# Macaron block on one core: the low parts of k and q ahead of the routing pieces, and ScalarE normalising the rows at the head of a batch's fifth step

## The reference

```python
def _layernorm(x, axis=-1, eps=1e-05):
    m = jnp.mean(x, axis=axis, keepdims=True)
    v = jnp.var(x, axis=axis, keepdims=True)
    return (x - m) / jnp.sqrt(v + eps)
...
# attention: 16 heads of 64; x is (8, 512, 128)
scores = jnp.einsum('bach,baCh->bacC', k, q)
masked = jnp.where(causal, scores, jnp.float32(-MASK_VAL))
attn = jax.nn.softmax(masked / np.float32(np.sqrt(D_HEAD)), axis=-1)
z = jnp.einsum('bacC,baCh->bach', attn, v)
out = jnp.einsum('aeh,bach->bce', W_O, z)
...
x = x + 0.5 * _L0_ffn_ref(_layernorm(x, axis=-1), ...)
x = x + _L0_attn_ref(_layernorm(x, axis=-1), ...)
x = x + 0.5 * _L0_ffn_ref(_layernorm(x, axis=-1), ...)
```

## Time and profile before

| | |
|---|---|
| Median of three runs | 929.5 us (927.78 to 931.06) |
| The profiled execution's own time | 929.25 us |
| Its span in the profile | 927.2 us |
| Busy share of the span | PE 96%, PEld 83%, DVE 84%, ACT 76%, POOL 30% |
| TensorE's granted clock | 0.995 of full speed on average |

### The profile page before, as it was taken

The page is one execution under the profiler, slowest core; times in us unless marked ns, Lnnn a source line. Parts: engine busy times, 40 slices in busy tenths (PEclk is TensorE's granted clock), DMA queues, the critical chain, the costliest instruction groups (busy, mean ns, idle before and its releaser), DMA issues.

```text
span 927.2 us, 25462 instructions
## 1 busy us (share of the span) xinstructions
PE 887.6 (96%) x7882; PEld 771.4 (83%) x7882; DVE 777.9 (84%) x3083; ACT 705.5 (76%) x2040; POOL 281.4 (30%) x328
## 2 busy tenths in 40 slices
PE   7999999979999999999999999999999998999995
PEld 6889999867887887887887887787788787999995
DVE  7878888779799889799889889979988986786666
ACT  3787667578887878787878787878887786887881
POOL 5777203142121021322222322310200202667552
PEclk9999999999999999999999999999999999999998
DMA  9677556155666575556456556554545454557758
GB/s 250 218 223 248 181 161 194 59 158 132 171 162 170 148 187 153 174 149 170 151 164 143 173 143 173 145 173 133 173 127 167 139 174 152 169 159 211 222 155 237
DMA packets 141300, 157.43 MB, mean 170 GB/s; under 512 B 35328, under 2 KB 108832, under 8 KB 141168
## 3 DMA queue, kind: packets, MB, share of 16 engines
q1 hardware_dynamic: 128256, 135.53, 50.1%
q0 software_dynamic: 8352, 18.17, 8.1%
q10 hardware_dynamic: 4560, 2.12, 0.8%
HBM read 97.53 MB, written 58.23 MB: 168 GB/s over the span
## 4 chain that ended last, share of the span: by engine, by line
PE 67%; DVE 15%; issue 6%; DMA 5%; POOL 3%; ACT 2%; SPq 2%; DVEq 0%; POOLq 0%; ACTq 0%
PE psum L2497 12%; PE psum L2382 8%; PE psum L2552 8%; PE psum L2538 7%; PE psum L2333 6%; PE psum L2335 5%; PE psum L2334 5%; PE psum L2561 5%; PE psum L2568 5%; DVE arena L1955 3%; POOL x_slots L852 2%; DVE arena L1970 2%; PE psum L2221 2%; PE psum L2355 1%; PE psum L2345 1%
## 5 line engine op out<-in xcount | busy, mean ns | idle before, releaser
L1125 ACT ACTIVATE arena<-arena,neg_max 128x512 f32<-128x512 f32 (+3 forms) x512 | 281.7, 554 | 108.2 <-DVE neg_max L1955 108.2
L1955 DVE CUSTOM_DVE_ANT_0 arena<-psum,causal 128x512 f32<-128x512 f32 (+3 forms) x512 | 217.1, 480 | 41.0 <-PE psum L2497 39.8
L1069 ACT ACTIVATE arena<-psum,b_t 128x256 f32<-128x256 f32 (+1 forms) x336 | 121.0, 443 | 38.8 <-PE psum L2335 29.2
L871 POOL DMA_INDIRECT arena<-y_tiles,y_at x64 | 61.7, 964 | 270.9 <-PE psum L2497 189.0
L2382 PE MATMUL psum<-w_sb,arena 128*128 x1136 | 140.8, 275 | 0.1
L2382 PEld LDWEIGHTS psum<-w_sb,arena 128*128 128x128 f32 x1136 | 134.2, 192 | 0.3 <-issue 0.3
L852 POOL DMA_INDIRECT x_slots<-xr,slot x64 | 62.1, 971 | 234.7 <-PE psum L2497 188.6
L2538 PEld LDWEIGHTS psum<-ident,arena 128*128 128x128 f32 x776 | 86.9, 141 | 17.8 <-ACT arena L1125 6.6
L2538 PE MATMUL psum<-ident,arena 128*128 128x128 f32 x776 | 95.9, 273 | 4.5 <-DVE arena L1985 4.1
L1135 ACT ACTIVATE arena<-psum 128x512 f32<-128x512 f32 x192 | 99.2, 587 | 0.6 <-PE psum L2538 0.6
L1125 ACT ACTIVATION_READ_ACCUMULATOR arena<-arena,neg_max 128x1 f32 x512 | 97.8, 191 | 0.0
(11 more groups left out here) (363 smaller groups left out, 2024.5 us busy)
## 6 DMA issues: line engine op xcount, KB each, us to landing
turned_dram<-arena SPq DMA_DIRECT2D x252, 128.0 KB
y_all<-turned_dram SPq DMA_DIRECT2D x63, 512.0 KB, 4.1
arena<-inv_dram SPq DMA_DIRECT2D x128, 128.0 KB, 3.9
w_raw<-in_L_ffn_W_dram SPq DMA_DIRECT2D x60, 256.0 KB
xg<-x_slots SPq DMA_DIRECT2D x43, 144.0 KB
arena<-in_L_ffn_W_dram SPq DMA_DIRECT2D x24, 256.0 KB
arena<-y_rows SPq DMA_DIRECT2D x16, 256.0 KB, 4.9
y_tiles<-y_all SPq DMA_DIRECT2D x27, 128.0 KB, 1.9
```

The source lines that it names most:

```text
L1069: ins = act.activation(h_t[side(f, n)][:, k, 0:rows], H_BANKS[side(f, n)][k // 2][:, k % 2 * rows:(k % 2 + 1) * rows], ACT.Relu, bias=b1_t ...
L1125: ins = act.activation(prob_tile(i, h, t), prob_tile(i, h, t), ACT.Exp, scale=-1.0, bias=neg_max[i % 2][:, h, t:t + 1], accum_out=row_sum[ ...
L1955: ins = dve.tensor_tensor_reduce(out=prob_tile(i, h, t), in0=score_tile(t, h), in1=causal[:, SEQ - (t + 1) * P:SEQ], scale=-1.0, scalar=-2 ...
```

## The change

The splits of the next step's k and q move ahead of the first four pieces of a step (in the step before the last, ahead of all that are finished there). `norms(b)` no longer normalises: it waits until ScalarE has read the values of the batch before, computes `moments` as before, and one product, `shift` = -mean x rstd. Step 3 finishes what is left. ScalarE normalises with activations of the kind Identity (scale `rstd`, bias `shift`), one for each tile of 128 rows, four tiles for `xa` and four for `xr1`, at the head of step 4, ahead of that step's exponentials.

```diff
-        TURN_STEP, PUT_STEP, JOIN_STEP = 4, 4, 5
+        TURN_STEP, PUT_STEP, JOIN_STEP, NORM_STEP = 4, 4, 5, 4
...
+            def normalise_rows(b, dst, col, ready):
+                for n in range(QT):
+                    ins = act.activation(dst[:, n, 0:D], xs[:, b * QT + n, :], ACT.Identity, bias=shift[:, col + n:col + n + 1],
+                                         scale=rstd[:, col + n:col + n + 1])
+                ins.then_inc(ready, 1)
+
+            def normalise_for(b):
+                act.wait_ge(norm_ready, U1 + b + 1)
+                if b + 1 < BATCH:
+                    normalise_rows(b + 1, xa[(b + 1) % 2], 0, xa_ready)
+                if b > 0:
+                    if b - 1 >= 2:
+                        act.wait_ge(x_put[b - 3], SCATTERED)
+                    normalise_rows(b - 1, xr1[(b - 1) % 2], QT, xr_ready)
...
+                    if s == NORM_STEP:
+                        normalise_for(b)
                     exps(i, 3)
...
                 if b > 0:
                     yield from measure(batch_of(b - 1), QT)
-                yield from moments(slice(0 if b + 1 < BATCH else QT, 2 * QT if b > 0 else QT))
-                if b + 1 < BATCH:
-                    yield from normalise(batch_of(b + 1), xa[(b + 1) % 2], 0, xa_ready)
                 if b > 0:
-                    yield from second_rows(b - 1, QT)
+                    dve.wait_ge(xa_ready, b + 1)
+                if b > 1:
+                    dve.wait_ge(xr_ready, BATCH + b - 1)
+                tiles = slice(0 if b + 1 < BATCH else QT, 2 * QT if b > 0 else QT)
+                yield from moments(tiles)
+                dve.scalar_tensor_tensor(out=shift[:, tiles], in0=mean[:, tiles], scalar=-1.0, in1=rstd[:, tiles],
+                                         op0=ALU.mult, op1=ALU.mult).then_inc(norm_ready, 1)
+                yield
...
                         turn_long(i)
+                    if i + 1 < STEPS:
+                        split_k(i + 1)
+                        split_q(i + 1)
                     if i == STEPS - 2:
                         finish(work)
                     go_on(work, 4)
-                    if i + 1 < STEPS:
-                        split_k(i + 1)
-                        split_q(i + 1)
...
                     go_on(work, 5)
+                    if s == NORM_STEP - 1:
+                        finish(work)
```

## The result

The changed kernel takes 939.62 us (median of four runs, 938.2 to 941.96), against 930.28 us of the kernel before (927.78 to 931.37): the ratio is 1.0107, 95% interval 1.0076 to 1.0137. It is 9.3 us slower. The profiled execution took 939.29 us beside a span of 937.6 us, that is 10.0 us over the profiled execution of before, where 7.8 us were forecast. The two spans differ by 10.4 us.

A forecast was written before the change was run, and what follows sets the result against it. Steps were taken as TensorE's own 8.88 us plus delays paced by a chain through three engines. 5 x 1.31 + 1.17 + 0.6 = 8.3 us, less 0.5, gave 7.8 over 929.25: 937.0 us, range 933 to 940.5.

The forecast's parts named there:

- What bounds the kernel: Step heads: 0.36 us is the ordinary cost of turning to the next step; only time beyond TensorE's 8.88 us is winnable.
- the 18.7 us: TensorE's weight loads, listed as waiting for q_lo in 35 places; rival (a) took these waits as real, faster, chance 0.08.
- ScalarE's block: Head of step 4, batches 1 to 6: eight activations overfill 1.66 us idle; 1.31 us a batch, 1.17 in batch 1.
- the two delays: Step 5's later scores (0.84 us) and later low part of activations (1.31 us); rival (c) had them add, 943 us, chance 0.06.
- VectorE's relief: VectorE loses 56 normalisations, 15.5 us in all; at most some 1.1 us in step 4, which the block holds longer anyway.
- The splits: VectorE's two subtractions ahead of up to four pieces: counted at nothing, at most 1.4 us gained, with a loss near the end.
- The 0.23 us of step 2: Batch 3: the part of TensorE's 0.60 us wait for q_lo that earlier splits free, but that isn't kept.
- so these come when they did: Steps 3 and 4: VectorE has no idle time before their maxima, so their starts, and step 4, stay unchanged.
- The step before the last: The rest of the routing falls behind the splits, delaying count_bf, last scores and last maxima; 0.6 us loss, between 0 and 1.2.
- Batches 0 and 7: Their four activations take 1.54 us and fit in idle time; both together counted at nothing, bounds -1.0 and +0.5.
- What would show it: Signs expected in the changed profile, among them step 4 0.8 us longer, step 5 0.5, and q_lo's sum down over 10 us.
- slower tiles: Upper bound of the range: ScalarE's block tiles taking 0.03 us more for each of 8 x 6, 1.4 us.

The follow-up runs named there:

- split_only: The kernel before with only the splits moved ahead of the four pieces, VectorE still normalising; 995.13 us, ratio 1.0036 to the kernel before.
- norm_only: The changed kernel with the splits put back behind the pieces, ScalarE still normalising; 998.94 us against 991.84 of the kernel before, ratio 1.0069.
- half: The changed kernel, but ScalarE normalises only the four tiles of xa and VectorE those of xr1; 992.38 us, ratio 1.0006 to the kernel before.
- two_steps: The changed kernel with ScalarE's tiles divided, xa heading step 4 and xr1 step 5 (batch 7: step 4); 991.74 us, ratio 0.9989 to the kernel before.
- twelve: The changed kernel with four more, unused activations at the head of step 4 in batches 1 to 6; 1007.68 us, ratio 1.0224 to the kernel before.
- spread: two_steps with the splits back behind the pieces and pieces redistributed over steps in batches 1 to 6; 976.69 us against 984.89 of the kernel before, 0.9915.
- after_again: The changed kernel, unchanged, profiled again on another chip; 995.13 us against 984.89 of the kernel before, ratio 1.0096.
- before_again: The kernel before, unchanged, profiled again as the control on the other chip; 986.36 us in one run.

## Why the prediction was right

**What bounds the kernel.** Right. The 0.36 us at the heads was the price of the turn; only the label went from q_lo to "issue". split_only shows that none of the 18.7 us could be had. The prediction says that nearly all of the 35 gaps are of that length: 25 are within 0.01 us of it. Of the other ten two are long, 2.7 and 2.0 us in steps 1 and 2 of batch 0, and the change left these as they were.

**ScalarE's block.** Right in mechanism and size. 0.385 us a tile and 3.08 us for eight, against 0.386 and 3.09; step 4's exponentials 4.07 us behind the head against 2.77, 1.30 us later (forecast 1.31). norm_only shows it by itself, 1.29 us a batch against 1.31, and half, two_steps and twelve bracket it: four tiles cost nothing, eight 1.3 us, twelve 1.53 us more. Steps 4 and 5 grew by 0.81 and 0.48 us, forecast 0.8 and 0.5, and as forecast the two delays didn't add. One reading beside it was wrong and without effect: the tiles of 506 to 509 ns in the earlier trace rows are said to stand where the other engines were busy, but the twelve that started between 26.3 and 31.1 us, where TensorE was busy all the time, took 479 to 483 ns. VectorE's relief was put at 15.5 us of busy time, and its busy time fell by 9.2 us; no term of the sum hangs on it, and the difference was not looked into.

**The splits.** The 0.23 us of step 2 came (9.68 to 9.45 us) and weren't kept, as forecast. The step that failed is "so these come when they did": I took VectorE's sum of work as free of its order. (By it the pieces, now behind the splits, still end where they did, and the maxima of steps 3 and 4 with them.) Step 3 grew by 0.39 and not by 0.23 us, because the chain of small operations lost an independent operation in its midst; that is 0.16 us a batch, and makes 1.45 of 1.31 us. This term of the sum was mis-sized at nothing, inside no bound that I gave, and six batches are 0.9 us more than forecast by it (8.6 against 7.7).

**The step before the last.** Right: 0.6 us forecast; the head of the last step is 0.32 us late and its maxima 0.26 us more. The rows of the changed kernel show count_bf behind the splits and TensorE waiting for it:

```profile
770.71 0.68 DVE L1959 TENSOR_TENSOR q_lo<-psum,q_hi 128x512 fp32r<-128x512 f32 x1
...
772.10 0.19 DVE L1357 TENSOR_TENSOR count_bf<-hot 128x32 bf16<-128x32 f32 x1
...
772.43 0.18 PE L2261 MATMUL psum<-count_bf,before_bf 128*128 128x32 bf16 x1 [0.92 <-DVE count_bf L1357]
```

**Batches 0 and 7.** I took 0.5 us off for them and the ends of the splits. That term has no basis: the text counts the splits and these batches at nothing, and the middle of their bounds is -0.95 us together, or -0.25 for the batches alone. Batch 7 lost 0.3 us outside of its end instead (steps 4 and 5: 10.28 and 9.40 against 10.20 and 9.18), and batch 0 with what lies ahead gained 0.1, the clock's 0.7 us in step 1 included. Steps 4 and 5 of batch 0 show the part that four normalisations less on VectorE and four more on ScalarE play: 19.35 us together against 19.66, and 19.19 against 19.68 on the second chip. Step 5 of batch 7 is 0.2 us longer in every kernel in which ScalarE writes xr1 there; why was not followed up.

**What would show it.** One sign came out short: the sum for q_lo fell by 5.4 us and not by over 10, because six heads of step 5, which wait for ScalarE's copies, carry its name with 8.0 us, and three heads of batch 0 keep 5.3 us.

**The sum and the range.** Between the forecast of 7.8 us and the 10.0 us of the profiled execution lie 2.2 us: 0.9 of the chain, 0.7 of batches 0 and 7 (0.2 lost where 0.5 was taken off), and 1.0 behind the last step's maxima, which didn't come again on the second chip, less 0.4 by which the time outside of the span fell. The range went up to 940.5, although the terms that are named for it reach 937.0 + 1.4 + 0.6 + 1.0 = 940.0. The measured 939.62 us lie inside, but its two large terms, slower tiles and a gain of the ends that doesn't come, are not what filled it: the tiles were not slower, and the chain had no bound. That the block sets the loss was forecast for the right reason; that the range held is in part luck.

## What to carry to other kernels

Idle time is a gap at a place: what an engine can take over is what fits between its last instruction and its next release, and the rest is paid by all who stand behind it in the queue. The share of the page (ScalarE 76%) says nothing of it, while one bracket of the timeline (1.66 us) does, and splitting a block over two gaps can turn a loss into nothing. A wait in the table that has the same length in steps where nobody is late is the price of the step, not a wait for the engine named. Relief for an engine brought nothing here where the rest of its work stayed in place (two_steps), and 8 us came with the work laid anew (spread); whether the new layout alone would have brought them was not tested.

## What the runs showed of the hardware

- Small dependent operations on VectorE (128x8) start 0.20 to 0.21 us apart, independent ones 0.08 us apart. A long independent operation behind a link of such a chain hides the difference, 0.12 us; with what else shifted, taking it out cost 0.16 us.
- In twelve, TensorE's loader was idle for 2.9 us at the head of step 5 in six batches. In four of them the granted clock was 0.50 for 3.4 us, beginning between 0.1 us ahead of the head and 2.3 us behind it, and step 5 was 0.4 to 1.6 us longer than in after_again; in two it stayed at 1.00, and the step was as long as there. Behind the changed kernel's stalls of 1.3 and 0.8 us it stayed at 1.00 in all six.
- In step 5 of batches 2 to 5 the update of TensorE's semaphore stands 1.15 us behind the end of its matmul in before_again and 1.45 us in after_again, and not on the first chip, with the same instructions and the clock at 1.00. Such late updates are in all traces of the three other chips, 0.6 to 0.7 us in spread and its kin. The cause stays open.
